# A two-layer mixture-of-experts kernel on one core: blank rows and part of the second layer's sends issued beside other stages, and the solver's rows computed in two alternating halves of the head columns

## The reference

```python
xn = _layernorm(x, axis=-1)
s = _L0_attn_ref(xn, ...)      # linear attention, output projection, layer norm
g = _silu(_L0_ffn_ref(xn, ...))  # top 2 of 8 experts, gelu, no capacity limit
x = x + s * g
xn = _layernorm(x, axis=-1)
s = _L1_attn_ref(xn, ...)
g = _silu(_L1_ffn_ref(xn, ...))  # top 2 of 8 experts, 1280 places each
x = x + s * g
```

```python
probs = jax.nn.softmax(logits + causal_mask, axis=-1)
L = jnp.eye(s) - jnp.tril(probs, -1)
rhs = jnp.diagonal(probs, axis1=-2, axis2=-1)[..., None] * v
A = jax.scipy.linalg.solve_triangular(L, rhs, lower=True)
```

## Time and profile before

| | |
|---|---|
| median of 3 runs | 1509.32 us (1508.48 to 1514.42) |
| the profiled execution's own time | 1505.75 us |
| its span, first to last instruction | 1504.0 us |
| mean granted TensorE clock | 0.805 of full speed |
| PE busy, PEld busy | 977.9 us, 763.0 us |
| DVE busy | 881.5 us in 2511 instructions |
| ACT busy, POOL busy | 466.8 us, 343.7 us |
| hardware DMA queue (SP), software DMA queue (POOL) | 143.79 MB, 19.02 MB |

### The profile page before, as it was taken

The page is one execution under the profiler, slowest core; times in us unless marked ns, Lnnn a source line. Parts: engine busy times, 40 slices in busy tenths (PEclk is TensorE's granted clock), DMA queues, the critical chain, the costliest instruction groups (busy, mean ns, idle before and its releaser), DMA issues. The chain is left out here.

```text
span 1504.0 us, 28696 instructions
## 1 busy us (share of the span) xinstructions
PE 977.9 (65%) x10762; PEld 763.0 (51%) x10762; DVE 881.5 (59%) x2511; ACT 466.8 (31%) x1066; POOL 343.7 (23%) x406
## 2 busy tenths in 40 slices
PE   5057499990565046767649967759977758967651
PEld 5036389980521034456535556536655646756541
DVE  5256373225778056656668866768857770057665
ACT  1123144434224003312125512125522217922114
POOL 0047445550047620012110012110002310013220
PEclk9978699995578578977679978679978868968776
DMA  9901288856149865510035420035521006521026
GB/s 230 240 33 53 69 239 246 230 140 164 31 64 246 252 140 133 144 33 27 13 71 141 128 71 26 13 98 140 138 63 37 26 12 178 157 72 32 14 67 168
DMA packets 256170, 164.65 MB, mean 109 GB/s; under 512 B 80960, under 2 KB 238912, under 8 KB 255776
## 3 DMA queue, kind: packets, MB, share of 16 engines
q1 hardware_dynamic: 246880, 143.79, 37.1%
q0 software_dynamic: 9152, 19.02, 3.9%
HBM read 99.12 MB, written 63.63 MB: 108 GB/s over the span
## 5 line engine op out<-in xcount | busy, mean ns | idle before, releaser
L1178 DVE TENSOR_REDUCE mx<-banks 128x1 f32<-128x384 f32 (+3 forms) x352 | 203.1, 636 | 62.0 <-PE banks L1110 61.6
L1332 DVE TENSOR_TENSOR prod<-A,Kst_Pn 128x16 f32<-128x16 f32 (+30 forms) x496 | 149.9, 302 | 25.3 <-POOL A L1288 8.4
L1336 DVE TENSOR_REDUCE A<-prod 128x8 f32<-128x16 f32 (+30 forms) x496 | 147.0, 296 | 17.0
L1158 ACT ACTIVATE Eoff_RT_hidden<-banks 128x256 f32<-128x256 f32 (+2 forms) x192 | 114.9, 599 | 102.4 <-PE banks L1095 93.3
L492 POOL DMA_INDIRECT rows_dram<-xr,slot x128 | 130.8, 1022 | 62.2 <-issue 38.6
L795 POOL DMA_INDIRECT o_dram<-step_o,step_to x80 | 78.8, 985 | 287.5 <-ACT step_o L784 275.3
L1106 PE MATMUL banks<-masks,identb 128*128 128x128 bf16 (+2 forms) x352 | 89.1, 253 | 75.8 <-DMA Qmax<-q_stack 66.9
L1093 PE MATMUL banks<-Qexp,Kst_Pn 128*128 128x256 bf16 x640 | 115.1, 282 | 35.5 <-DMA Qmax<-q_stack 28.7
L1160 ACT ACTIVATE Ed<-banks 128x256 f32<-128x256 f32 x256 | 97.9, 382 | 122.5 <-PE banks L1095 122.5
L1283 POOL TENSOR_TENSOR A<-A,Kst_Pn 128x256 f32<-128x256 f32 x16 | 14.2, 890 | 498.0 <-DVE Rb L1319 462.0
L1110 PE MATMUL banks<-Kst_Pn,Qmax 128*128 128x128 bf16 (+3 forms) x512 | 121.6, 308 | 0.0
(11 more groups left out here) (181 smaller groups left out, 1690.4 us busy)
## 6 DMA issues: line engine op xcount, KB each, us to landing
Kst_Pn<-k_stack SPq DMA_DIRECT2D x32, 512.0 KB, 4.6
rows_dram<-blank SPq DMA_DIRECT2D x12, 858.0 KB, 11.0
e_w<-in_L_w1T_dram SPq DMA_DIRECT2D x39, 256.0 KB
e_w<-in_L_w2T_dram SPq DMA_DIRECT2D x39, 256.0 KB
c_r<-o_dram SPq DMA_DIRECT2D x32, 256.0 KB, 5.3
sum_dram<-Eoff_RT_hidden SPq DMA_DIRECT2D x32, 256.0 KB, 3.8
Qmax<-q_stack SPq DMA_DIRECT2D x64, 96.0 KB
Qexp<-q_stack SPq DMA_DIRECT2D x64, 96.0 KB
```

The costliest lines, as they stand in the source:

```text
L1158: nc.scalar.activation(Eoff[:, n % 4, 0:I, :, :].rearrange("p j h q -> p (j h q)"), big[n % n_big][:, 0:I * 2 * P], ACT.Exp, scale=scale)
L1178: nc.vector.tensor_reduce(out, logits, AX_X, ALU.max, negate=True).then_inc(max_done, 1)
L1332: nc.vector.tensor_tensor(prod[:, :, 0:r + 1], A[:, :, k0:k0 + r + 1], Pn[:, c * SUB + r:c * SUB + r + 1, 0:r + 1].broadcast_to([P, HD, r ...
L1336: nc.vector.tensor_reduce(A[:, :, k0 + r], prod[:, :, 0:r + 1], AX_X, ALU.add).then_inc(row_done, 1)
```

## The change

Three parts. First, the twelve blank writes for the second layer are issued by SP in `linear_attention` (new `blank_second`) and no longer in the first `normalise`. Second, of the second layer's 64 sends 36 stay in `project_qkv`, and the other 28, with the wait for the landing of all, are issued by POOL at the end of its list in `attend(-1)`; for that the sent rows, their places and two semaphores live on in the tile `Ed`, which the solver first writes later, and the set of tiles and semaphores named `second` is gone; the first three `load_rows` move from the block at L957 into `solve_block(0)`. Third, the solver's rows are computed in two halves of four features each: product 0, product 1, sum 0, sum 1, each waiting only for the last instruction of its own half.

```diff
--- before.py
+++ after.py
@@ -207,6 +208,10 @@
         def _(pool):
             send(pool)
+
+        @block.sync
+        def _(sp):
+            blank_second(sp)
 
...
@@ -484,14 +489,14 @@
 
 
-def send_rows(nc, pool, rows, slot, rows_dram, rows_set, n_set, sent):
+def send_rows(nc, pool, rows, slot, rows_dram, rows_set, n_set, sent, which):
 
     pool.wait_ge(rows_set, 16 * n_set)
-    for k in range(2):
-        for t in range(NT):
-            nc.gpsimd.indirect_dma_start(rows_dram, bass.IndirectOffsetOnAxis(slot[:, k, t:t + 1], 0),
-                                         rows[k][:, t, :], None).then_inc(sent, 16)
-    pool.wait_ge(sent, 16 * 2 * NT)
+    for k, t in (divmod(n, NT) for n in which):
+        nc.gpsimd.indirect_dma_start(rows_dram, bass.IndirectOffsetOnAxis(slot[:, k, t:t + 1], 0),
+                                     rows[k][:, t, :], None).then_inc(sent, 16)
+    if which.stop == 2 * NT:
+        pool.wait_ge(sent, 16 * 2 * NT)
 
...
@@ -960,8 +964,6 @@
                 for i in range(2):
                     steps.load_expert(sp, i)
-                for k in range(steps.NX):
-                    steps.load_rows(sp, k)
 
...
@@ -1019,6 +1021,7 @@
                 pool.wait_ge(one_cleared, 1)
                 nc.gpsimd.memset(one[:, HD:HD + 1], 1.0)
+                send_rest(pool)
 
...
@@ -1217,8 +1220,7 @@
                 if k % steps.PER_EXPERT == 0 and k >= 2 * steps.PER_EXPERT:
                     steps.load_expert(sp, k // steps.PER_EXPERT)
-                if k >= steps.NX:
-                    steps.load_rows(sp, k)
+                steps.load_rows(sp, k)
 
...
@@ -1326,14 +1328,18 @@
                 k0 = t0 + c * SUB
                 for r in range(1, SUB):
-                    n = ops * c + 2 * (r - 1)
-                    if r > 1:
-                        dve.wait_ge(row_done, n)
-                    nc.vector.tensor_tensor(prod[:, :, 0:r + 1], A[:, :, k0:k0 + r + 1],
-                                            Pn[:, c * SUB + r:c * SUB + r + 1, 0:r + 1].broadcast_to([P, HD, r + 1]),
-                                            ALU.mult).then_inc(row_done, 1)
-                    dve.wait_ge(row_done, n + 1)
-                    nc.vector.tensor_reduce(A[:, :, k0 + r], prod[:, :, 0:r + 1], AX_X, ALU.add).then_inc(row_done, 1)
+                    n = ops * c + 4 * (r - 1)
+                    for i in range(2):
+                        if r > 1:
+                            dve.wait_ge(row_done, n - 1 + i)
+                        ds = slice(i * HD // 2, (i + 1) * HD // 2)
+                        nc.vector.tensor_tensor(prod[:, ds, 0:r + 1], A[:, ds, k0:k0 + r + 1],
+                                                Pn[:, c * SUB + r:c * SUB + r + 1, 0:r + 1].broadcast_to([P, HD // 2, r + 1]),
+                                                ALU.mult).then_inc(row_done, 1)
+                    for i in range(2):
+                        dve.wait_ge(row_done, n + 1 + i)
+                        ds = slice(i * HD // 2, (i + 1) * HD // 2)
+                        nc.vector.tensor_reduce(A[:, ds, k0 + r], prod[:, ds, 0:r + 1], AX_X, ALU.add).then_inc(row_done, 1)
                 ks = slice(c * SUB, (c + 1) * SUB)
...
@@ -1437,7 +1443,11 @@
         rows1_dram = nc.dram_tensor("rows1_dram", (E * CAP + P, ROW), F32).ap()
         o1_dram = nc.dram_tensor("o1_dram", (2 * T + SPARE * P, D), F32).ap()
-        wt1 = sb("wt1", [P, 2, NT])
+        wt1, slot1 = sb("wt1", [P, 2, NT]), sb("slot1", [P, 2, NT], U32)
+        rows1_set, sent1 = sem("rows1_set"), sem("sent1")
+        Ed = sb("Ed", [P, BH * P])
+        xr1 = [Ed[:, k * NT * ROW:(k + 1) * NT * ROW].rearrange("p (t c) -> p t c", c=ROW) for k in range(2)]
+        xnT1 = Ed[:, 2 * NT * ROW:2 * NT * ROW + T]
         x_dram = nc.dram_tensor("x_dram", (B, L, D), F32).ap()
...
@@ -1475,6 +1481,8 @@
                             sp.dma_start(rows_dram[i * SPARE * P:(i + 1) * SPARE * P].rearrange("(n p) c -> p n c", p=P),
                                          blank[:, :, :]).then_inc(rows_set, 16)
+
+                    def blank_second(sp):
                         for i in range(0, E * CAP // P, SPARE):
...
@@ -1514,15 +1522,16 @@
                         sp.dma_start(dst, more[n]).then_inc(w_in, 16)
 
-                slot1, eid1 = sb("slot1", [P, 2, NT], U32), sb("eid1", [P, NTL], U32)
+                eid1 = sb("eid1", [P, NTL], U32)
                 route(nc, "g1_", CAP, xr1, slot1, wt1, eid1, {**const, **made}, bank, qkv_weights)
                 project_qkv(nc, xnT1, wT, wsT, bias, rot, w_in, bank, k_stack, q_stack, vT_dram,
-                            lambda pool: send_rows(nc, pool, xr1, slot1, rows1_dram, rows1_set, 0, sent1))
+                            lambda pool: send_rows(nc, pool, xr1, slot1, rows1_dram, rows1_set, N_SET, sent1, range(SENDS)))
         Apos = ctx.enter_context(nc.sbuf_tensor("Apos", [P, (LT * BH) * (HD + 1) + 32], F32))
         with ExitStack() as layer:
             sb, _ = tensors(nc, layer)
             A = sb("A", [P, HD, L])
-            solve_attention(nc, A, Apos, rows1_dram, o1_dram, more, k_stack, q_stack, vT_dram, max_dram, sum_dram)
+            solve_attention(nc, A, Apos, Ed[:, :].rearrange("p (l q) -> p l q", q=P), rows1_dram, o1_dram,
+                            lambda pool: send_rows(nc, pool, xr1, slot1, rows1_dram, rows1_set, N_SET, sent1, range(SENDS, 2 * NT)), more, k_stack, q_stack, vT_dram, max_dram, sum_dram)
         with ExitStack() as layer:
```

More of the change, by code:

```diff
@@ L50 @@
 SPARE = 13
+SENDS = 36
 N_SET = -(-E * CAP // P // SPARE) + -(-2 * NT // SPARE)
@@ L181, in _, with linear_attention @@
                 nc.scalar.copy(xnT[:, g * L:(g + 1) * L], bank[g % 2][:, :]).then_inc(copied, 1)
-def linear_attention(nc, xn, xnT, s, rows, mv, rstd, wk, wqv, wo, w_in, ident, bank, send):
+def linear_attention(nc, xn, xnT, s, rows, mv, rstd, wk, wqv, wo, w_in, ident, bank, send, blank_second):
     with ExitStack() as ctx:
@@ L913, in _, with solve_attention @@
             lowest(B - 1)
-def solve_attention(nc, A, Apos, rows_dram, o_dram, w, k_stack, q_stack, vT_dram, max_dram, sum_dram):
+def solve_attention(nc, A, Apos, Ed, rows_dram, o_dram, send_rest, w, k_stack, q_stack, vT_dram, max_dram, sum_dram):
     bank, big, ident = w["bank"], w["big"], w["ident"]
@@ L937, in solve_attention @@
         Qexp = [sb(f"Qexp{i}", [P, NH, P], BF16) for i in range(2)]
-        Ed = sb("Ed", [P, BH, P])
         shared = sb("Eoff_RT_hidden", [P, 4 * 2 * L])
@@ L978, in solve_attention @@
             attend(nc, I, A, vT_dram, ident, Kst, Qmax, Qexp, k_stack, q_stack, max_dram, sum_dram, mx, mxp, mxT,
-                   masks, identb, Ed, Eoff, Apos, one, RT, Rb, bank, big)
+                   masks, identb, Ed, Eoff, Apos, one, RT, Rb, bank, big, send_rest)
             if I >= 0:
@@ L984, in attend @@
 def attend(nc, I, A, vT_dram, ident, Kst, Qmax, Qexp, k_stack, q_stack, max_dram, sum_dram, mx, mxp, mxT, masks,
-           identb, Ed, Eoff, Apos, one, RT, Rb, bank, big):
+           identb, Ed, Eoff, Apos, one, RT, Rb, bank, big, send_rest):
     now, ahead = I >= 0, I + 1 < LT
@@ L1202, in solve_block @@
     per_sub = SUB // TURN
-    ops = 2 * (SUB - 1)
+    ops = 4 * (SUB - 1)
     half = 4 * P
@@ L1448, in program @@
         with ExitStack() as second:
-            sb, sem = tensors(nc, second)
-            xr1 = [sb(f"xr1_{k}", [P, NT, ROW]) for k in range(2)]
-            xnT1 = sb("xnT1", [P, T])
-            rows1_set, sent1 = sem("rows1_set"), sem("sent1")
             with ExitStack() as layer:
@@ L1495, in program @@
                     linear_attention(nc, xn, xnT, s, rows, mv, rstd, wk, wqv, wo, w_in, ident, bank,
-                                     lambda pool: send_rows(nc, pool, xr, slot, rows_dram, rows_set, 6, sent))
+                                     lambda pool: send_rows(nc, pool, xr, slot, rows_dram, rows_set, 6, sent, range(2 * NT)), blank_second)
                 routed_experts(nc, "e0_", eid, rows_dram, o_dram, w["L0_w1T"], w["L0_w2T"], w["L0_b1T"], w["L0_ffn_b2"],
```

## The result

| | before | after |
|---|---|---|
| median | 1508.9 us (1504.64 to 1514.42, 4 runs) | 1442.87 us (1441.68 to 1444.59, 4 runs) |
| the profiled execution's own time, span | 1505.75, 1504.0 us | 1442.47, 1440.6 us |
| DVE busy | 881.5 us in 2511 instructions | 866.7 us in 3503 |

A second set of runs gave 1443.26 us and 0.958 (0.9551 to 0.9609).

The account below looks back on a forecast made before the run. Stages were taken as bounded by the list ending last, no engine throughout. Terms -29.2 - 7.5 - 1.5 - 1.0 + 9.4 - 21.3 = -51.1 against 1505.75 gave 1454.7; with 3.57 added, median 1458 us, range 1447 to 1480.

Parts of the forecast that it names:

- blank writes: First normalise: routing starts at 35.8 us instead of 65.0, -29.2 us, with nothing given back in linear_attention.
- project_qkv: sends, clearing: project_qkv: 28 sends leaving free DMA time for SP's queue, -7.5 us; one semaphore set less to clear, -1.0 us.
- attend(-1): attend(-1): POOL's list with the 28 sends becomes the last of the stage, +9.4 us (8.5 to 9.9).
- solver's rows: solve_block: halves save 1.97 us per chunk; first chunks 5.5, second nothing, third and fourth 15.8, together -21.3 us.
- from the profiled execution to the median: Whole kernel: the profiled execution lay 3.57 us below the median, so 3.57 was added to the forecast.
- Rival (c): linear_attention: sends stall while moved blank writes fill the DMA engines, stage up to 30 us later, 1488; chance 0.06.
- Rival (b): Sends in attend(-1) take 1133 ns (+5) and SP's queue in project_qkv gets no relief (+7.5): 1470; chance 0.10.
- 579.4 ... a few tenths for the barrier follow: End of attend(-1): last send landed at 579.4 us on the old clock, with only a few tenths until the next stage.
- I take 80, near the two of the kinds closest to the row chain: Solver's rows on DVE: an independent instruction starts 80 ns before the one ahead ends, saving 1.97 us per chunk.
- My own upper bound, 2.9 us per chunk: Solver's rows: with 90 ns of overlap a chunk saves 2.9 us, 29 in all.
- rival (a): Solver's rows: overlap nearer 65 ns, as in the seven maxima, so -3 in place of -21.3: 1476; chance 0.17.
- rival (d): Solver's row chain: no overlap, each row 387 ns and each chunk 12.0 us more, time 1664, slower; chance 0.05.

Follow-up runs that it names:

- run 3: Kernel before with only the twelve second-layer blank writes moved into linear_attention: 1477.46 us, ratio 0.9801.
- run 7: Changed kernel with 3, 2, 2 and 3 expert steps per block in place of 3, 3, 2 and 2: 1438.11 us, ratio 0.9544.
- run 2: Kernel before with only the solver's rows computed in halves: 1474.52 us, ratio 0.978.
- run 8: Kernel before with 3, 2, 2 and 3 expert steps per block: 1507.52 us, ratio 1.0006.
- run 5: Changed kernel with all 64 second-layer sends back in project_qkv: 1438.58 us, ratio 0.9555.
- run 10: Changed kernel with 44 sends in project_qkv, 20 in attend(-1), and 3, 2, 2, 3 expert steps: 1429.15 us, ratio 0.9483.
- run 4: Changed kernel with each row's instructions reordered to product and sum of half 0, then of half 1: 1546.18 us, ratio 1.0237.
- run 12: Changed kernel with rows in four groups of two features instead of two of four: 1548.06 us, ratio 1.027.
- run 9: Changed kernel itself, unaltered, measured again: 1443.26 us.
- run 11: Changed kernel with 44 sends in project_qkv, 3, 2, 2, 3 expert steps, last two sends issued in the next solver block: 1424.6 us, ratio 0.9456.

## Why the prediction was right and wrong

| term | forecast | in the two traces |
|---|---|---|
| blank writes | -29.2 | -29.4 |
| project_qkv: sends, clearing | -7.5, -1.0 | -9.7 |
| loads out of the short block | -1.5 | -1.6 |
| attend(-1) | +9.4 | +11.55 |
| solver's rows | -21.3 | -30.1 |
| everything else | 0 | -4.2 |
| sum | -51.1 | -63.4 |
| from the profiled execution to the median | 3.57 | 0.40 |

**Blank writes: right**, in place and size. Rival (c), sends that stall beside them, fell with 980 ns per send and a stage of 114.02 us against 114.09, and run 3 by itself gave its 30.8.

**linear_attention: the last list misread, at no price.** The prediction had DVE end this stage, 0.8 us behind the last landing. The 14 profiled executions say POOL: the next stage starts 7.9 to 8.1 us after the end of the last send in every one of them, while from DVE's end it is anything from 4.9 to 9.1 us. In run 7 DVE is done before the last send is even issued:

```profile
141.16 0.35 DVE L371 RECIPROCAL yrstd<-yrstd 128x32 f32<-128x32 f32 x1 [0.30 <-ACT yrstd L307]
```

```profile
141.74 0.96 POOL L496 DMA_INDIRECT rows_dram<-xr,slot  x1 [0.30 <-issue]
```

```profile
150.65 0.36 SPq L532 DMA_DIRECT2D e_xt<-rows_dram  x1
```

So the sends bind here, and there was no cover at all; the blank writes cost nothing because POOL's time per send stayed as it was.

**project_qkv: the mechanism right, the clearing not shown.** SP's list ends 485.19 - 397.89 = 87.3 us after the stage's start instead of 95.1, 7.8 less. Its queue's share rose by 16.3 points, where the sends' queue gave up 19.5 (21.2% to 1.7%). From SP's end to the next block it is 4.25 us instead of 6.17, but that is no price of a clearing: in runs 2, 3 and 8, where this stage is as in the kernel before, it is 4.78, 6.65 and 5.03. Run 5, with all the sends here and one clearing less, takes 100.35 us to the short block, and the four executions with the stage of before 100.3 to 101.3. So most of the 9.7 is the sends', and what a clearing costs stays open. The basis of its bounds falls too, since the 4.85 us of the earlier trace rows begin at the end of DVE, which isn't last there. Rival (b) fell on both of its halves, since the sends in attend(-1) took 966 ns, not 1133.

**attend(-1): the mechanism right, the tail mis-sized.** The step "579.4 ... a few tenths for the barrier follow" failed. The next stage starts 539.92 - 535.31 = 4.6 us after the last send's end; I had 2.3 plus some tenths. Runs 7 and 10 show 2.8 us behind an indirect send even in blocks where nothing waits for its landing, so it is not the landing alone. In the earlier trace rows stood the warning: 7.9 us lie there between the last send's end and the next stage, and I gave them to DVE's end and the clearings. How such a tail divides between landing, clearing and the rest no run shows.

**Rows: the step that failed.** "I take 80, near the two of the kinds closest to the row chain" was the term of the sum that was mis-sized. DVE's row chain fell from 20.65 us per chunk to 17.64 (means of the 16), so by 3.01, not 1.97, and what an instruction costs less behind an independent one is 95 ns by the model above. The overlap itself is near the 80 assumed (74 to 85 ns in the traces); the step missed that the instruction also gets shorter by some 15 ns. My own upper bound, 2.9 us per chunk, was about right. The 65 of the seven maxima of the earlier trace rows, on which rival (a) stood, is a mean that one wait for PE pulls down. The first five take

```profile
584.92 3.08 DVE L1178 TENSOR_REDUCE mx<-banks 128x2 f32<-128x512 f32 x5
```

which is 0.60 us from start to start where each lasts 0.684, an overlap of 86 ns; the sixth starts 0.73 us after the fifth. The right direction was shown by runs 4 and 12: rival (d), no overlap, is what run 4 does for the pairs that depend on each other. Its price stood in the prediction as 387 ns per row against whole rows; run 4, which leaves out half of the overlaps, cost 0.26 us per row against the changed kernel and made it slower than before.

The Trainium skill ("VectorE: DVE Perf Modes", section "The DRAIN you can't avoid") has the next instruction wait until the pipe is empty, with a semaphore or without, but adds "A next op that is not held starts earlier"; the prediction gave only the first half. For independent instructions the trace agrees with the addition alone: 0.19 us from a sum to an independent product where the sum lasts 0.28. For dependent ones the first half fits, with 0.31 against 0.27.

**Where the gain fell, by chunks.** The third and fourth gave 26.7 instead of 15.8, for 3.01 per chunk makes 24.1. The rest fits turn_rows, which is faster once the wait ahead of it is short: in the third chunks 1.08, 1.75, 1.66 and 1.08 us instead of 1.94 each, 2.2 in all. The second gave 2.7 instead of nothing, 1.7 of it in block 0, where an expert step's matmuls took 2.05 us instead of 3.77. The first gave 0.7 instead of 5.5: PE's wait was not free time in that execution, because the clock rose a step later. Run 9 shows that this is the execution's and not the kernel's.

**The rest.** 4.2 us lie in stages that no edit touches. One profile of each kernel can't carry that: between the two profiles of the changed kernel the same stages moved by up to 1.4 us each. And the 3.57 us from profiled execution to median, which I carried over, were 0.40 after. Both together are 7.3 of the 15 us. The runs bear the parts out without them: 33.7 (run 2) and 30.8 (run 3) make 64.5 of the 66. The sends with all that goes with them are left with 1.5, which is less than the intervals resolve; run 5 shows it of the split alone.

The solver's rows (8.8 us), the untouched stages (4.2), the carried offset (3.2) and project_qkv (1.2) lie below the forecast, the tail of attend(-1) (2.15) above it; that is the 15 us. The range took 90 ns of overlap and the semaphores as its lower end, with no room for scatter from one execution to the next on top.

## What to carry to other kernels

On DVE, what a chain of small dependent instructions costs is set by the order as much as by the count: against whole rows two independent halves in alternation gained 34 us here, the same instructions half by half lost 69, and four groups lost about as much. What to count is the spacing of starts (64 ns if independent and 194 if not, with 1.03 per element here), not the durations. After a chain gets shorter, redistribute the work beside it: three expert steps in the last chunk were worth nothing before; after, they took 11.5 us out of the second chunks, though only 3 to 5 us by the medians reached the end and the intervals don't separate that from none. And look at which list ends a stage, by the distance that stays the same over several executions: an indirect send at the end of POOL's costs 3 to 5 us that no instruction shows, and 7.9 in linear_attention.

## What the runs showed of the hardware that I had not expected

- An independent DVE instruction starts 74 to 85 ns before the end of the one ahead and, in the changed kernel, lasts some 15 ns less than the same shape did before (269 against 283 ns at 120 elements). Four groups hide no more than two (run 12).
- The next stage starts 2.8 us after the end of an indirect send that is last in POOL's list (4.6 where its landing is waited for), but 0.75 us after a DVE copy. Two sends moved to the next block took 3.1, 3.1 and 1.6 us out of the ends of three blocks (runs 10 and 11).
- Sends of 128 rows keep their time on POOL while SP's writes fill the DMA engines (980 ns against 981), but land 6.4 us after the issue instead of 2.3.
- TensorE's granted clock rises from 0.50 to 1.00 at one of two places in a solver block's first chunk, and which one changes from one execution to the next: the first step's 16 matmuls into `down` take 2.05 or 3.78 us. With halves the chunk takes 27.4 to 27.6 or 29.3 to 29.4 us (run 9); with whole rows it took 29.5 either way.
